# Decoder layer on one core: operand parts in the second operand buffer, memory turned beside the first maxima

## What is computed

```python
def attn(x):                      # 16 heads of 8
    q, k, v = x @ W_q, x @ W_k, x @ W_v
    latent = (k + v) @ W_down_kv  # width 32
    k_rec, v_rec = latent @ W_up_k, latent @ W_up_v
    scores = q k_rec^T / sqrt(128) * exp(-0.01 * |t - s|)
    return softmax(scores) @ v_rec @ W_o

def xattn(x, memory, mask):       # memory: 6404 rows of 128, one head
    q = x @ W.T + b
    logits = q @ memory.T + (1 - mask) * -1e6
    return softmax(logits) @ memory

def ffn(x):                       # width 352, operands rounded in blocks of 16 to a 4-bit grid
    return fp4_linear(silu(fp4_linear(x, w_gate)) * fp4_linear(x, w_up), w_down)

x = x + attn(layernorm(x)); x = x + xattn(layernorm(x), memory, mask); x = x + ffn(layernorm(x))
```

## Time and profile before

| | kernel before |
|---|---|
| median of 3 runs | 531.59 us (530.63 to 531.82) |
| profiled execution, its span | 529.92 us, 528.1 us |
| PE busy | 489.9 us, 93% |
| DVE busy | 361.1 us, 68% |
| ACT busy | 335.8 us, 64% |
| POOL busy | 173.0 us, 33% |
| chain that ended last, by engine | PE 77%, DVE 14%, ACT 3%, DMA 3% |

### The profile page before, as it was taken

The page is one execution under the profiler, slowest core; times in us unless marked ns, Lnnn a source line. Parts: engine busy times, 40 slices in busy tenths (PEclk is TensorE's granted clock), DMA queues, the critical chain, the costliest instruction groups (busy, mean ns, idle before and its releaser), DMA issues.

```text
span 528.1 us, 9777 instructions
## 1 busy us (share of the span) xinstructions
PE 489.9 (93%) x3480; PEld 319.0 (60%) x3480; DVE 361.1 (68%) x858; ACT 335.8 (64%) x659; POOL 173.0 (33%) x292
## 2 busy tenths in 40 slices
PE   7349899999999999998997999999999999999997
PEld 6205433333232333333444999989898989999996
DVE  6889989887878787861445446676767677565354
ACT  5635777778787878787656484746547373747531
POOL 6820023544544444333454222231232332310000
PEclk9857999999999999999999999999999999999999
DMA  8987300025003500003269543524243433410000
GB/s 239 297 263 146 71 22 3 2 64 119 3 2 66 116 4 2 3 1 122 62 166 334 164 145 94 157 57 160 59 156 91 132 114 92 138 42 1 6 6 6
DMA packets 27956, 49.22 MB, mean 93 GB/s; under 512 B 4140, under 2 KB 15860, under 8 KB 27332
## 3 DMA queue, kind: packets, MB, share of 16 engines
q1 hardware_dynamic: 27156, 47.87, 32.7%
q0 software_dynamic: 224, 0.54, 0.3%
q10 hardware_dynamic: 528, 0.18, 0.2%
HBM read 43.67 MB, written 4.72 MB: 92 GB/s over the span
## 4 chain that ended last, share of the span: by engine, by line
PE 77%; DVE 14%; ACT 3%; DMA 3%; issue 2%; POOL 1%; SPq 0%; DVEq 0%; POOLq 0%; ACTq 0%
PE banks L981 52%; PE banks L1090 12%; PE banks L1246 7%; DVE banks L807 6%; PE banks L1101 2%; DMA operands<-query_parts 1%; DVE fa L918 1%; DVE fb L919 1%; ACT logits L683 1%; DMA x_sb<-in_x 1%; ACT probs L672 1%; PE banks L1153 1%; DMA query_parts<-operand_parts 1%; PE banks L1299 1%; DVE fa L917 1%
## 5 line engine op out<-in xcount | busy, mean ns | idle before, releaser
L672 ACT ACTIVATE probs<-banks 128x512 f32<-128x512 f32 x288 | 160.2, 599 | 49.1 <-PE banks L981 43.5
L807 DVE CUSTOM_DVE_ANT_0 banks<-banks,decay 128x1024 f32<-128x1024 f32 x128 | 155.1, 1244 | 31.3 <-PE banks L981 30.7
L981 PE MATMUL banks<-operands 112*128 112x512 bf16 (+4 forms) x736 | 148.3, 332 | 20.8 <-DMA operands<-query_parts 13.9
L981 PEld LDWEIGHTS banks<-operands 115*128 115x128 bf16 (+1 forms) x736 | 55.3, 98 | 126.5 <-ACT probs L672 55.1
L981 PEld LDWEIGHTS banks<-mem,pT 128*128 128x128 f32 (+1 forms) x816 | 105.6, 191 | 7.8 <-ACT pT L693 0.2
L981 PE MATMUL banks<-mem,pT 128*128 128x128 f32 (+1 forms) x816 | 109.5, 276 | 0.0
L693 ACT ACTIVATE pT<-banks 128x512 f32<-128x512 f32 (+1 forms) x104 | 60.4, 581 | 55.8 <-PE banks L1246 55.8
L883 DVE CUSTOM_DVE_ANT_0 logits<-banks,mring 128x512 f32<-128x512 f32 (+1 forms) x85 | 56.0, 667 | 39.7 <-PE banks L981 30.1
L535 POOL TENSOR_SCALAR_AFFINE_SELECT probs<-probs 128x128 f32<-128x128 f32 x128 | 37.3, 294 | 108.9 <-ACT probs L672 107.0
L1090 PE MATMUL banks<-probs,v_ext 128*32 128x512 f32 x512 | 68.2, 605 | 0.1
L1246 PE MATMUL banks<-ident,logits 128*128 128x128 f32 (+1 forms) x408 | 61.9, 274 | 0.0
(11 more groups left out here) (169 smaller groups left out, 499.2 us busy)
## 6 DMA issues: line engine op xcount, KB each, us to landing
mring<-in_mask_BxSxS_ik SPq DMA_DIRECT2D x39, 512.0 KB, 3.5
operands<-key_parts SPq DMA_DIRECT2D x24, 192.0 KB
operands<-query_parts SPq DMA_DIRECT2D x21, 192.0 KB
key_parts<-operand_parts SPq DMA_DIRECT2D x10, 256.0 KB, 3.5
mem<-in_ctx SPq DMA_DIRECT2D x3, 832.0 KB, 9.2
mask<-in_mask_BxSxS_ik SPq DMA_DIRECT2D x9, 256.0 KB, 3.0
pT<-in_mask_BxSxS_ik SPq DMA_DIRECT2D x9, 256.0 KB, 3.1
query_parts<-operand_parts SPq DMA_DIRECT2D x4, 384.0 KB, 5.0
```

Of the source, the lines that this page charges most:

```text
L672: act.activation(probs[:, to, :], PS[:, u % 3, :], ACT.Exp).then_inc(s_p, 1)
L807: dve.tensor_tensor_reduce(out=rows, in0=rows, in1=decay[:, off:off + S], scale=1.0, scalar=-3.0e38, op0=ALU.mult, op1=ALU.max, accum_out= ...
L981: return pe.matmul(o, a, b, start=start, stop=stop, skip_group_check=alone)
```

## The change

`parts_sb` now lies in `operands_1`. So ScalarE's copies into `memT_hi` wait for no stores, and POOL, which sets the constant rows of `operands_1`, waits for all of them; the loads into `operands_1` wait for POOL. PE turns the first three memory chunks ahead of the first maximum, as soon as all operands are scaled (`s_scaled`), and one chunk in each of the turns 0 to 9; `mem_rest` stands in the turns 0 to 12. Turns 15 to 21 end with five transposes of the identity each. The fill has 22 turns. The six shift DMAs of the first group are shared by SP (QL) and ACT (QU). The feed-forward weights are read by POOL once the first operands are there. The scales of these weights are made ahead of units 46, 64 and 80, and POOL quantizes them in pairs 7 to 27.

```diff
--- before.py
+++ after.py
@@ -61,11 +61,12 @@
     BLKS = NH * NT
     PAIRS = NG * BLKS // 2
     PU = 2 * HG + 1
-    MAX_LEAD = 7
+    MAX_LEAD = 6
+    MEM_FIRST = 3
+    FILL_WARM = 5
     MEM_FRONT = 19
-    SCALE_UNITS = (28, 36, 44)
-    QUANT_PAIR = 3
-    MEM_UNIT = 8
+    SCALE_UNITS = (46, 64, 80)
+    QUANT_PAIR = 7
     MEM_LAG = 2
     EARLY_PAIR = PAIRS - 4
     EARLY_J = 4
@@ -117,7 +118,6 @@
             iota_i = sb0("iota_i", [P, S], I32); iota_d = sb0("iota_d", [P, 2 * S - P], I32)
             mem_front = sb0("mem_front", [P, MEM_FRONT, D])
             sb0("pad_first", [P, NK * P - 4 * S + P - MEM_FRONT * D])
-            parts_sb = sb0("operand_parts", [P, 4, PARTS, S], BF16)
         memT_lo = sb("memT_lo", [P, NK * P], F32R)
         memT_hi = sb("memT_hi", [P, NK * P], F32R)
         qc = sb("qc", [P, 2, P])
@@ -136,6 +136,8 @@
             v_ext = sb1("v_ext", [P, NT, HEADS, VW])
             decay = sb1("decay", [P, 2 * S - P])
         OPB = 4 * HG * S // 2
+        parts_sb = ops[1][:, :, :, :].rearrange("p w h n -> p (w h n)")[:, 0:4 * PARTS * S].rearrange(
+            "p (w i n) -> p w i n", w=4, i=PARTS)
         logits_0 = sb("logits_0", [P, S2])
         pT = sb("pT", [P, 3, BANK]); sb("pad_0", [P, OPB - S2 - 3 * BANK])
         mem = sb("mem", [P, NK, D])
@@ -306,6 +308,12 @@
         def up_bank(t):
             return 6 if t == NT - 1 else 7
 
+        def store_shift(eng, hg, w):
+            for i in range(PARTS):
+                row = queries(hg // NH % NB, w, hg % NH)[SHIFT_ROW + i:SHIFT_ROW + i + 1, :, :]
+                eng.dma_start(row.rearrange("p h (t q) -> p (h t) q", q=P),
+                              shift_parts[:, i, :]).then_inc(s_sh[hg % 2], 16)
+
         def store(sp, t):
             sp.wait_ge(s_f12, t + 1)
             sp.dma_start(out[0, t * P:(t + 1) * P, :], x_sb[:, t, :]).then_inc(s_out, 16)
@@ -382,13 +390,10 @@
                              mask[0, t * P:(t + 1) * P, m * MP:m * MP + w]).then_inc(s_mk[n % NRING], 16)
 
             def load_shift(hg):
-                g, half = hg // NH, hg % NH
                 sp.wait_ge(s_sp, hg + 1)
-                for w in (QL, QU):
-                    for i in range(PARTS):
-                        row = queries(g % NB, w, half)[SHIFT_ROW + i:SHIFT_ROW + i + 1, :, :]
-                        sp.dma_start(row.rearrange("p h (t q) -> p (h t) q", q=P),
-                                     shift_parts[:, i, :]).then_inc(s_sh[hg % 2], 16)
+                store_shift(sp, hg, QL)
+                if hg > 0:
+                    store_shift(sp, hg, QU)
 
             sp.dma_start(mem_front[:, :, :], ctx[0, 0:MEM_FRONT * P].rearrange("(t p) d -> p t d", p=P)).then_inc(s_mf, 16)
             sp.dma_start(mem_back[:, 0:NKF - MEM_FRONT, :],
@@ -471,6 +476,7 @@
             pool.memset(v_ext[:, :, :, HD:HD + 1], 1.0).then_inc(s_vclear, 1)
             pool.wait_ge(s_vclear, 1)
             link(pool.memset(wg_raw[FF - NKW * P:P, :, :].rearrange("p (a n) d -> p a n d", a=2)[:, :, NKW, :], 0.0))
+            pool.wait_ge(s_op0, 16 * 2 * PARTS)
             pool.dma_start(wd_raw[:, :], w_down).then_inc(s_fw, 16)
             for i, w in enumerate((w_gate, w_up)):
                 full = FF // P
@@ -481,6 +487,9 @@
 
 
             pool.wait_ge(s_iota2, 1)
+            pool.wait_ge(s_scr0, 16)
+            for w in range(4):
+                pool.wait_ge(s_scr[w], 16 * (SLOTS if w in (KL, KU) else 1 if w == QL else NH))
             for w, value in ((KL, ONES_PAIR), (QL, 0.0), (QU, 0.0), (KU, ONES_PAIR)):
                 pool.memset(spare_rows(1, w), value).then_inc(s_spare[1], 1)
             pool.wait_ge(s_spare[1], 4)
@@ -620,10 +629,6 @@
             def mem_high(c):
                 k0, kw = chunk(c)
                 act.wait_ge(s_mt, c + 1)
-                if c == 0:
-                    act.wait_ge(s_scr0, 16)
-                    for w in range(4):
-                        act.wait_ge(s_scr[w], 16 * (SLOTS if w in (KL, KU) else 1 if w == QL else NH))
                 act.activation(memT_hi[:, k0:k0 + kw], PS[:, c % 4, 0:kw], ACT.Copy).then_inc(s_mhi, 1)
 
             def mem_low(c):
@@ -636,6 +641,8 @@
                     mem_high(step)
                 if step >= MEM_LAG:
                     mem_low(step - MEM_LAG)
+            act.wait_ge(s_sp, 1)
+            store_shift(act, 0, QU)
 
             def take_oT(half):
                 act.wait_ge(s_pu, NT // 2 * (half + 1))
@@ -1196,13 +1203,19 @@
                 if early_logits(s) is not None:
                     logits(early_logits(s))
 
+            pe.wait_ge(s_scaled, NH * 4)
+            for step in range(MEM_FIRST):
+                mem_tiles(step)
             for mu in range(UNITS + MAX_LEAD):
                 max_turn(mu)
-                step = mu - MEM_UNIT
-                if 0 <= step < NC:
-                    mem_tiles(step)
-                if MEM_LAG <= step < NC + MEM_LAG:
-                    mem_rest(step - MEM_LAG)
+                if mu < NC:
+                    mem_rest(mu)
+                if mu + MEM_FIRST < NC:
+                    mem_tiles(mu + MEM_FIRST)
+                if mu == NC + MEM_LAG:
+                    pe.wait_ge(s_mlo, NC)
+                if mu >= NC + MEM_LAG:
+                    keep_warm(FILL_WARM)
             pe.wait_ge(s_mlo, NC)
             for n in range(PAIRS):
                 mu = UNITS + MAX_LEAD + 4 * n
```

## The result

| | kernel before | changed kernel |
|---|---|---|
| median of 5 runs each | 531.58 us (529.07 to 531.82) | 525.9 us (525.77 to 527.14) |
| ratio of the two | | 0.9911 [0.9886, 0.9935] |
| profiled execution, its span | 529.92 us, 528.1 us | 525.9 us, 524.0 us |
| PE, DVE, POOL busy | 489.9, 361.1, 173.0 us | 491.4, 361.8, 172.4 us |

The change is faster by 0.9%. The forecast was 528.0, range 525.7 to 530.7. In the profiled execution 4.1 us of span are gone, where 3.6 were forecast. I went through the changed kernel with the views used before, in the order of the program.

The account below looks back on a forecast made before the run. DVE was taken to bound the fill, PE the pairs from 64 us on. Fill -1.2 (extra unit included), change of group -2.6 and last shift rows +0.2 sum to -3.6 us: 531.6 to 528.0, range 525.7 to 530.7.

Parts of the forecast that it names:

- Start of the fill: First maxima up to the split: clock full at 35.0, split ending at 55.25 instead of 55.66, 0.4 us gained.
- End of the fill: PE free of DVE one maximum earlier, behind unit 22, at 62.4 instead of 63.97: 1.6 us gained, start's 0.4 included.
- Granted clock 1.00 to 62: Expected sign in the fill: clock full before 36 us and at 1.00 from there to 62.
- sign of being wrong: The forecast is wrong if the clock's row shows 0.5 between 45 and 60 us.
- rival B: Clock falls once in the fill, after idle time in turns 13 and 14: +1.5 to 2.2 us, 530.0; chance 16%.
- Change of group: Pairs: a `pv` between dependent units removes PE's 0.51 us wait for DVE at six changes: -2.6 us.
- the weight scales: DVE's scales ahead of units 64 and 80 take back 0.2 us at each of two changes of group.
- One unit more in the pairs: A unit moved from the fill into the pairs, where PE is the bound: 0.4 us lost.
- The last shift rows: First scores of pair 28: PE waits 0.8 us for late rows, less 0.6 it waited for ScalarE anyway: +0.2.
- The edits counted at nothing: POOL's memsets, the loads behind them, moved weight reads and quantizing, and first shift rows on two queues: no cost.
- The step from the profile to the median: Median of before lies 1.7 us above its profiled execution; this carries over, so 526.3 profiled means 528.0.

Follow-up runs that it names:

- e1: Kernel before with only MAX_LEAD 6 instead of 7, the last remainder then standing behind the fill: 527.34 us, ratio 0.9943.
- e4: Changed kernel with memory work back at turns 8 to 22, no identity transposes, three shift DMAs still on ScalarE's queue: 537.8 us, ratio 1.0146.
- e7: As e4, but all six shift DMAs of the first group on SP: 527.71 us, ratio 0.9964.
- e8: Kernel before with 16 and 4 identity transposes behind the fourth and fifth logits chunks, ahead of the wait for `cmax`: 528.29 us, ratio 0.9976.
- e2: Changed kernel with MAX_LEAD back at 7, all other edits kept: 529.52 us, ratio 0.9986.
- e5: Changed kernel with the five identity transposes in turns 13 and 14 as well: 526.84 us, ratio 0.9955.
- e6: Changed kernel with POOL reading the feed-forward weights near 18 us again, without waiting: 526.77 us, ratio 0.9946.
- e9: Changed kernel timed again, unchanged, in a later series: 526.97 us, ratio 0.9944.
- e10: Changed kernel with the edits of e5 and e8, and the last group's maxima turned three scores earlier: 525.98 us, ratio 0.9928.
- e11: Changed kernel with weight scales ahead of units 28, 36 and 44 and quantizing in pairs 3 to 23, as before: 526.71 us, ratio 0.994.
- e12: Changed kernel with all six shift DMAs of the first group on SP: 527.28 us, ratio 0.9951.

## Why the prediction was right, step by step

**Start of the fill: the number right, partly by luck.** The clock was to be full before 36 and the split to end at 55.25. It was full from 34 and the split ended at 55.25. Two errors of the working cancelled: the clock rose 1 us earlier than the 35.0 that I took (0.4 gained), and fell once more (0.4 lost). And that the 0.4 against before are the change's is not shown: the split ends at 54.66 to 56.25 in the five profiles with the memory turned late (before, e1, e4, e7, e8), and at 54.29 to 55.60 in the nine with it early.

**End of the fill: right, size and reason.** PE was to be free of DVE at 62.4; unit 22, the last one that it waits for, starts at 61.19 and takes 1.2. The mark is at -1.44 for -1.6. The split is 0.4 of it and the way from there to the `pv` 1.03 (12.17 to 11.14). e1 and e2 show what it takes: with the memory early and 23 turns it is 12.16, with 22 turns and the wait for `memT_lo` 11.52. Where the fall at 51 does nothing behind the split (e5, e6, e9, e10) it is 10.98, so 1.18 to 1.19 less than with 23 turns: one maximum, as worked out. I had worked out that this wait isn't what the path goes through; that holds with 23 turns and no longer with 22, so two edits share this term.

**"Granted clock 1.00 to 62": wrong.** The prediction's own sign of being wrong, 0.5 between 45 and 60, is in the rows, and rival B's event took place: turns 13 and 14, with 0.6 us of work in 1 us, stood ahead of a fall of the clock at 51. Its price was not 1.5 to 2.2 us but 0.5 (and 0.8 at most in e6, e11 and e12). I had PE's turns of 1.9 stand on the path for two or three turns. In fact PE was the slower one for one unit: DVE had the tile of the next unit full already when the clock fell, DVE takes no unit from PE during the split (1.2 us), and the clock was up at 54.4, behind PE's unbroken work from 50.39 on, most of it transposes. That the idle time of these two turns is what brings the clock down fits e5 and e10, which fill it and have no fall; but e2 and e9 have the idle time and no fall either.

The Trainium skill, "TensorE: Matmul & The Clock Gate", section "A second HAM failure mode: psum-queue depth-cycling", had spoken for such a fall at short idle times of PE. This trace agrees as to the fall; e2 and e9, in which the clock stayed at 1.00 through the same turns, don't.

**Change of group: the mechanism right, the size too large.** Four pairs with the first change take 92.19-66.39 = 25.80, as forecast. Over six changes it is 2.03 us, from -1.44 to -3.47 at the `pv` of 228.24 (231.71 before), instead of 2.6. Two things make the difference. A change by itself is worth 26.25-25.80 = 0.45, not 0.5: 6 x 0.45 = 2.70. And the weight scales take back 0.17 + 0.27 + 0.25 = 0.69 at three changes, where 0.4 at two were counted (e11). 2.70 - 0.69 = 2.01. In the list of waits the scales don't show, because PE's runs of matmuls there are stretched and no idle time of its own is recorded; the first of these is the same work in pair 1 and in pair 5:

```profile
75.09 1.26 PE L988 MATMUL banks<-operands 115*128 115x256 bf16 x7
...
100.89 1.43 PE L988 MATMUL banks<-operands 115*128 115x256 bf16 x7
```

e2 brings back all six waits and the 1.4 us.

**One unit more in the pairs, 0.4 lost: half of it.** At 233.73 the difference is -3.27, so 0.2.

**The last shift rows, +0.2: 0.4.** The wait is 0.66 where I had 0.8, and the difference goes from -3.27 to -2.87 at 239.42. I set ScalarE's 0.6 against it in full; not all of it lay at the same place. e10 takes the wait out and gains 0.1, so the true loss lies between. The rows for the other groups were on time, as worked out.

**The edits counted at nothing: right.** The weights' reads cost nothing that a run shows (e6), and no row of PE waits for the memsets (they start at 41.08, where I had 38.5) or for SP's loads behind them; no run moves them alone. The scales were counted in the term above; against their old place the new one costs 0.17.

**Sum.** Worked out again by terms: -1.4 -2.0 +0.2 +0.4 = -2.8, where the forecast had -1.2 -2.6 +0.2 = -3.6 with the extra unit in the first. The span shows -4.1 because the late fall of the clock, 1.3 us, was in the execution of before and not in that of the changed kernel. e9, with the fall in both, has -3.1 of span, and medians 2.8 us apart. So the first measured gain of 5.7 us was partly a high median of before (531.58, later 529.7) and a low one of the changed kernel (525.9, later 526.97). The forecast's ratio, 0.993, lies between the two measured ones.

The step from the profile to the median failed: before's median lay 1.7 us above its profiled execution, and I let that carry over. The changed kernel's median, 525.9, is its profiled execution's time. This and the late fall, not a larger effect of the change, brought the median 2.1 us below the forecast and to 0.2 us from the lower end of the range, which I had put there for another reason (all of the excess of the changes of group gone). That it still lies inside is luck.

**What the rest of the change does** is little. I had 0.4 for it, the earlier split; e2 shows 0.64 at one mark, no more than profiles of one fill differ by, and a ratio whose interval holds 1; e1, the one number, has 0.9943 where all edits have 0.9944, and both intervals leave room for 1 us. The earlier memory saves the wait for `memT_lo` but takes away the work that kept the clock up; the identity transposes give that back; the second queue saves 0.3.

What stays open: why a change of group gives back 0.45 of the 0.51 that PE waited; whether the earlier memory work gains anything; and which executions have the clock's falls at 51, at 252 and behind the wait for `cmax`. The traces show that identical programs differ there; in both profiles in which the idle time ahead of `cmax` is filled (e8, e10) the last fall is absent. Nothing shows what decides.

## What to carry to other kernels

Where a producer feeds a consumer through two buffers, look at the turn in which the order is broken (a unit left out, then two at once): moving it by one place so that another engine's long work lies between the dependent units was worth more than all of the moved memory work. Look also at what else the other engine does just ahead of that turn: the same weight scales cost nothing in the old order and 0.5 to 0.7 us in the new one. Ask of each edit of a large change whether it is its own gain or repairs another edit's loss, and test the smallest of them alone. When a run prices a moved step, first see that the queue behind it hasn't moved too; and before a difference is explained from two profiles, compare both at marks in stretches that the change doesn't touch.
